# Two chained cross-attentions: transposes of x' in two parts, banks of the second and third picked keys exchanged, second queries copy before the normalisation of tiles 0 and 1

## What is computed

```python
# L0: 16 heads of 16 channels, 64 context rows; token t sees only the rows idx[t]-1, idx[t], idx[t]+1
q = split(rmsnorm(x, gamma_q) @ Wq.T); kn = rmsnorm(ctx, gamma_kv)
k = split(kn @ Wk.T); v = split(kn @ Wv.T)
w = where(|pos - idx| <= 1, relu(q k / sqrt(16))**2, 0)
x1 = x + (w / max(w.sum(), 1e-6) @ v) @ Wo.T
# L1: one head, softmax over 64 context rows, then residual and layer norm
q = gelu(x1' @ Wq + bq); k = gelu(ctx @ Wk + bk); v = gelu(ctx @ Wv + bv)
out = layernorm(softmax(q k) @ v @ Wf + bf + x1) * ln_gamma + ln_beta
```

## Time and profile before

| | |
|---|---|
| median of 3 runs | 343.87 us (343.45 to 344.19) |
| profiled execution | 343.76 us, of which 342.0 us is the span from first to last instruction |
| busy in the span | PE 324.4 (95%), DVE 287.9 (84%), ACT 250.8 (73%), POOL 231.9 (68%) |
| 60 to 302 us (steps 3 to 16) | PE 239.1 of 242.0 us busy, clock share 1.00 |

### The profile page before, as it was taken

One profiled execution on the slowest core, in us unless ns is written; L12 is line 12 of the kernel. 1 busy time (PEld: TensorE's weight loads), 2 busy tenths in 40 slices (PEclk: granted clock), 3 DMA queues, 4 the chain that ended last, 5 costly groups with the idle time before them and its releaser, 6 DMA issues.

```text
span 342.0 us, 5710 instructions
## 1 busy us (share of the span) xinstructions
PE 324.4 (95%) x1914; PEld 238.7 (70%) x1914; DVE 287.9 (84%) x456; ACT 250.8 (73%) x598; POOL 231.9 (68%) x233
## 2 busy tenths in 40 slices
PE   8999999999999999999999999999999999989980
PEld 3675678868686767776768687776768686857750
DVE  2789598888888888898988888898888888889766
ACT  4898524587878787969696969697887878785752
POOL 4416170246979696969788787878797969665414
PEclk9999999999999999999999999999999999999996
DMA  6987635934253433425261616162624242110103
GB/s 234 389 249 201 196 109 128 252 83 140 76 184 93 167 110 141 137 105 172 71 207 61 216 61 213 66 202 76 183 94 161 103 150 91 52 61 0 63 0 123
DMA packets 30268, 46.34 MB, mean 136 GB/s; under 512 B 2400, under 2 KB 16736, under 8 KB 30240
## 3 DMA queue, kind: packets, MB, share of 16 engines
q1 hardware_dynamic: 27264, 37.86, 36.0%
q0 software_dynamic: 2016, 7.34, 5.3%
q10 hardware_dynamic: 960, 0.79, 0.7%
HBM read 25.14 MB, written 8.39 MB: 98 GB/s over the span
## 4 chain that ended last, share of the span: by engine, by line
PE 76%; DVE 18%; issue 3%; ACT 2%; DVEq 0%
PE ps L532 12%; PE ps L533 12%; PE ps L534 12%; PE ps L583 7%; PE ps L577 6%; DVE qkp L1339 5%; PE ps L668 4%; PE ps L785 4%; PE ps L776 4%; PE ps L703 4%; PE ps L617 2%; PE ps L564 2%; DVE kv L1257 2%; PE ps L673 1%; PE ps L517 1%
## 5 line engine op out<-in xcount | busy, mean ns | idle before, releaser
L1293 DVE TENSOR_TENSOR qkp<-ps,bufs 128x1024 f32<-128x1024 f32 x48 | 56.0, 1219 | 9.3 <-ACT bufs L1035 8.0
L443 POOL TENSOR_TENSOR bufs<-bufs,lng_twice 128x1024 f32<-128x1024 f32 x14 | 33.7, 2408 | 27.2 <-ACT bufs L1074 25.1
L432 POOL TENSOR_TENSOR qkp<-qkp 128x1024 f32<-128x1024 f32 x15 | 35.9, 2396 | 21.6 <-DVE qkp L1304 21.6
L389 POOL TENSOR_TENSOR x_lo<-x_ring,x_hi 128x1024 fp32r<-128x1024 f32 x16 | 38.2, 2387 | 7.0 <-ACT x_hi L1031 7.0
L1112 ACT ACTIVATE xp_hi<-bufs 128x512 fp32r<-128x512 f32 x28 | 17.7, 634 | 31.9 <-DVE bufs L1381 31.9
L1304 DVE TENSOR_TENSOR qkp<-ps,wn 128x1024 f32<-128x1024 f32 x31 | 37.6, 1215 | 3.8 <-PE ps L583 3.7
L448 POOL TENSOR_TENSOR bufs<-bufs,lnb_row 128x1024 f32<-128x1024 f32 x14 | 33.5, 2395 | 0.1
L1035 ACT ACTIVATE bufs<-ps 128x512 f32<-128x512 f32 x32 | 19.2, 602 | 14.4 <-PE ps L534 14.4
L532 PE MATMUL ps<-x_hi,wh_q 128*128 128x512 f32 x64 | 26.7, 417 | 0.0
L1042 ACT ACTIVATE bufs<-bufs 128x256 f32<-128x256 f32 x64 | 25.7, 407 | 0.0
L1074 ACT ACTIVATE bufs<-ps,nbias,half_rstd 128x256 f32<-128x256 f32 x52 | 25.2, 566 | 0.3
(11 more groups left out here) (257 smaller groups left out, 920.2 us busy)
## 6 DMA issues: line engine op xcount, KB each, us to landing
x_ring<-xT SPq DMA_DIRECT2D x16, 512.0 KB, 3.4
bufs<-x SPq DMA_DIRECT2D x16, 512.0 KB, 5.0
out<-bufs POOLq DMA_DIRECT2D x14, 512.0 KB, 3.3
idx_ring<-idx SPq DMA_DIRECT2D x16, 256.0 KB, 4.1
wkv_lo<-kv SPq DMA_DIRECT2D x32, 126.0 KB
kvs<-kv SPq DMA_DIRECT2D x30, 126.0 KB
vfd<-bufs SPq DMA_DIRECT2D x8, 256.0 KB, 4.7
qkp<-ctxT SPq DMA_DIRECT2D x2, 512.0 KB, 6.7
```

The costliest lines, as they stand in the source:

```text
L389: G.tensor_tensor(x_lo[:, :, :], x_ring[:, e % RING, :, :], f32_view(x_hi[:, :, :]), ALU.subtract).then_inc(xl_ready, 2)
L432: G.tensor_tensor(att[:, 1, :, :], att[:, 0, :, :], att[:, 1, :, :], ALU.add).then_inc(pair_ready, 1)
L443: G.tensor_tensor(zo, zn, lng_twice[:, :].unsqueeze(1).broadcast_to([P, TT, D]), ALU.mult).then_inc(zg_ready, 1)
L1293: V.tensor_tensor(qk[:, s, :, :], ps[:, bank0:bank0 + 2, :], q0, ALU.mult).then_inc(qk_ready, 1)
```

## The change

Four edits, for the batches after the first:

- UP keys go to banks 0 and 1 and DOWN keys to 6 and 7. The waits follow the banks: UP keys wait for the weighting of the DOWN values (`att_ready`), DOWN keys for the normalisation (`zn_ready`).
- DVE's products read from the exchanged banks.
- The eight transposes of x' become two calls of `back`: tiles 0 and 1 (bank 6) ahead of the `scT` transposes, tiles 2 and 3 (bank 7) behind them. The first call now waits for the third key product (`3 * a + 3`) and no longer for the second.
- On ACT the copy of the second half of the first queries (`copy_q0(a, 1)`, L1035) stands ahead of the normalisation of tiles 0 and 1 and no longer behind it.

```diff
             def up_keys(a):
                 pe.wait_ge(kvs_in[a % 2], 64 * (a // 2 + 1))
-                picked_keys(a, UP, 6)
+                picked_keys(a, UP, 6 if a == 0 else 0)
...
+                def back(tiles):
+                    for j in tiles:
+                        for c in range(DC):
+                            mm(out_rows(j, c * P, P), xpT[:, c, j * P:(j + 1) * P], ident,
+                               is_transpose=True, start=(j % 2 == 0 and c == 0), stop=False, skip_group_check=True)
+
                 if b is not None:
                     queries1(0)
                 if a is not None:
-                    if n is not None:
-                        pe.wait_ge(zn_ready, 2 * n + 2)
-                    if f == 0:
-                        pe.wait_ge(k1_copied, 4)
+                    pe.wait_ge(att_ready, 3 * f + 2)
                     up_keys(a)
...
                 if a is not None:
-                    pe.wait_ge(att_ready, 3 * f + 2)
-                    picked_keys(a, DOWN, 0)
+                    if n is not None:
+                        pe.wait_ge(zn_ready, 2 * n + 2)
+                    if f == 0:
+                        pe.wait_ge(k1_copied, 4)
+                    picked_keys(a, DOWN, 6)
...
                     if a is not None:
-                        pe.wait_ge(qk_ready, 3 * a + 2)
+                        pe.wait_ge(qk_ready, 3 * a + 3)
                     else:
                         pe.wait_ge(zn_ready, 2 * n + 2)
-                    for j in range(TT):
-                        for c in range(DC):
-                            mm(out_rows(j, c * P, P), xpT[:, c, j * P:(j + 1) * P], ident,
-                               is_transpose=True, start=(j % 2 == 0 and c == 0), stop=False, skip_group_check=True)
+                    back((0, 1))
                     pe.wait_ge(scT_cp, b + 1)
                     for u in range(2):
                         i = nc.tensor.transpose(ps[:, 4, (2 + u) * P:(3 + u) * P], scT[:, u * P:(u + 1) * P], ident)
                     i.then_inc(sc_mm, 1)
+                    back((2, 3))
...
                 if n is not None:
                     normalise(range(2, TT))
-                if n is not None:
-                    normalise(range(0, 2))
                 if a is not None and f is not None:
...
                     copy_q0(a, 1)
+                if n is not None:
+                    normalise(range(0, 2))
...
                     multiply_keys(a, CENTRE, 2)
-                    multiply_keys(a, UP, 6)
-                    multiply_keys(a, DOWN, 0)
+                    multiply_keys(a, UP, 0)
+                    multiply_keys(a, DOWN, 6)
```

## The result

| | before | changed |
|---|---|---|
| median of 4 runs | 343.66 us (343.30 to 344.19) | 340.93 us (340.88 to 341.43) |
| ratio | | 0.9923 (95%: 0.9905 to 0.994) |
| profiled execution | 343.76 us, span 342.0 | 340.88 us, span 339.1 |

The median fell by 2.7 us where 2.4 were forecast. POOL's lines, L610 and L668 kept theirs.

What follows compares the result with a forecast made beforehand. PE was taken as the bound, losing 0.29 us a step at L668 to DVE's sum. 13 x 0.17 = 2.2 plus 0.15 in the tail make 2.4 us: 343.76 to 341.4 us, range 340.6 to 342.2 (chance 0.62).

Steps and rivals of the forecast that it cites:

- The wait at L668: PE loses 0.29 us a step waiting for DVE's sum; the split makes L668 0.17 us earlier a step.
- new stop: PE reaches the `scT` transposes before their copy is ready: 0.06 us wait plus 0.06 restart a step.
- The first rival: The gap at L668 is the cost of changing from 32 to 128 columns, not DVE's sum: 343.8 to 345.4 us.
- The third: Rival: the split is worth more because `scT` doesn't delay PE, 339.8 to 340.5 us; chance of more than forecast 0.05.
- The exchange and the copy at nothing: Bank exchange worth nothing by itself; ACT's earlier query copy gives back 0.10 us, swallowed in a 0.11 cover: value 0.
- POOL: POOL's sequence comes 0.26 us late each step but loses that again at L419 behind DVE's instruction: cost 0.
- signs of being wrong: Steps of 17.88 or more; L403 without idle time and L419 at 0.20; L1339 waiting for L432; L577's load waiting for L1304.
- The fourth rival: POOL becomes the bound if over about 0.5 us late at L419: 344.9 us; slower through POOL or PE's wait 0.09.
- The second rival: Late POOL L416 holds up DVE's L1384, delaying UP keys up to 0.1 us a step: 342.7 us, chance 0.05.
- The tail: After step 16 L802 stands in L668's place; ACT, idle 0.16 before rounding the transposed sums, gains that: 0.15 us.
- The cover of the copy's 0.49: POOL's sum L432, 0.49 us later, still ends 0.15 before L1339 wants it, with 0.14 more beyond that.

Runs made afterwards that it cites:

- kernel 5: The changed kernel with five of the eight x' transposes ahead of the `scT` transposes and three behind: 339.98 us, 0.9884 of the kernel before the change.
- kernel 1: The kernel before the change with the split of the transposes alone, banks, waits and ACT's order as they were: 340.69 us, ratio 0.9928.
- kernel 3: The changed kernel with ACT's copy of the queries again behind the normalisation of tiles 0 and 1: 340.97 us, 0.9938 of the kernel before the change.
- kernel 8: The changed kernel with two extra small POOL additions a step (0.31 us) ahead of L403: 342.07 us, 0.995 of the kernel before the change.
- kernel 9: The changed kernel with five extra small POOL additions a step (0.78 us) ahead of L403: 352.22 us, 1.0242 of the kernel before the change.
- kernel 7: The kernel before the change with the split and the copy ahead of the normalisation, but no exchange of banks: 346.56 us, ratio 1.0075.
- kernel 4: The changed kernel with POOL's one-time doubling of ln_gamma moved ahead of the first normalisation factors: 340.66 us, 0.9924 of the kernel before the change.
- kernel 2: The changed kernel with all eight x' transposes again ahead of the `scT` transposes: 343.46 us, 1.0011 of the kernel before the change.
- kernel 12: The changed kernel run once more, unaltered: 341.44 us, 0.9933 of the kernel before the change.

## Why the prediction was right, and where it was not

**The wait at L668.** Right in place and size. The distance from the first x' transpose to L668 fell by 2.96 - 2.78 = 0.18, where 0.17 was worked out. The `scT` pair's new stop was forecast at 0.06 + 0.06. Undisturbed, the pair would start 0.17 + 3 x 0.11 = 0.50 behind the first of the four transposes; it starts 193.05 - 192.50 = 0.55 behind, and the next transposes 0.28 behind it in place of 0.22: 0.05 + 0.06. That L668 could start at L610's modelled end, without its own price for the change of width, was taken from one row and holds (0.08 before the end). The first rival, in which the gap is the price of the width, is refuted, since the gap went from 0.22 to nothing at the same change of width. The third is refuted too: `scT` does delay PE, and kernel 5 shows what the split gives without that delay.

**The exchange and the copy at nothing.** Right in the steady steps. Kernels 1 and 3 reach 17.67 without the copy. DVE's gain ahead of the first product stops at the third, which waits 0.51 for the DOWN keys.

**POOL.** Right for the steady steps. L419 was forecast to start 0.26 behind DVE's instruction and to end 0.74 behind its start; it starts 0.25 and ends 0.74 behind. Of the signs of being wrong one was there by half (L403 has lost its idle time in the steady steps, but L419 is at 0.49 and not at 0.20) and one in a single step (L1343 waits for L432). The fourth rival, POOL as the bound, had its point of decision right in kind: kernel 8 stands about on it at 17.67, kernel 9 beyond. But its price was too low: when POOL passes the first half of DVE's pair it doesn't lose only the excess, it runs into the second half or puts L416 behind the first, and loses another 0.5. The second rival, L416 holding up DVE, didn't come about: in the step above L416 runs from 184.87 to 185.91, L1388 starts at 185.74, inside it, and its pair takes 1.48 as ever.

**The tail.** Forecast 0.15, measured 0.24. The other kernels with a split have 55.36 to 55.48, apart from kernels 7 and 9, which are slower there too, so some 0.2 to 0.3 are real. What is beyond the 0.15 I haven't traced.

**Terms that were missed.** Two, of opposite sign, and they cancel in the sum. That the sum came out as near as it did is luck to this extent, some 0.4 us either way.
First, the first normalising step was taken to be like the others. The cover of the copy's 0.49 was worked out in a steady step (0.15 before L1339, then 0.14), and the doubling L439, once 0.69 with its start, was not on the list. That step takes 18.17 where 17.71 had been counted: 0.46, and kernel 4 takes it away.
Second, each steady step is 17.67 and not 17.71, 11 x 0.04 = 0.4 us more gain. The difference doesn't lie where the change was costed: 0.18 of the 0.22 are between the x' transposes and L668, and the other 0.04 are between L668 and the next x' transposes, in matmuls whose order didn't change. Kernel 1 has it without the exchange or the copy, and kernel 2 without the split. Half of it, 0.02 in the mean, arises in the first matmuls L532 and L533 behind the UP keys. There the weight load waited 0.19 for the copy L1035, which the prediction put at nothing because loads run ahead. In the changed kernel and in kernel 2 this wait is gone. But kernel 1 still has it (2.4 us in 13 places) and has steps of 17.67 all the same, so it isn't shown to be the cause. What makes these distances shorter stays open.
With -0.43 at the start of the program, which is of the run and not of the change, the numbers close: 13 x 0.17 + 0.15 = 2.4 forecast; 2.45 measured behind the start, and 2.7 to 2.9 over all. The repeat on another chip, kernel 12, gave 343.52 - 341.44 = 2.1, so tenths of these differences of medians aren't to be read.

The Trainium skill (SBUF — State Buffer, "Who interferes with whom") says that a DVE instruction with two SBUF inputs and a POOL instruction which reads SBUF keep each other out until the one that began first has ended. Where DVE was first the rows agree that POOL is held up: 0.73 and 0.49 for 0.20 at L419, and 1.57 for 1.04 at L416 in kernel 9. They don't show it shut out until DVE has ended: L419 ends with DVE's instruction and not 0.20 behind it, and L416 loses 0.53 and not 0.72. Where POOL was first, L416 ahead of L1388, they don't, and the measurement decides: DVE wasn't held up.

## What to carry to other kernels

Where an engine that is the bound waits for a result, look at the chain that produces it: if the engine itself makes an early link of that chain and stands behind filler work, move just as much filler behind the link as lets its input be ready when the engine comes to it. Here the right cut was 5 and 3 of 8, worth 4.2 us, while 4 and 4 left a stop and 6 and 2 delayed the result again. A cover that is worked out in a steady step must be checked in the first and last ones, where work that is done once comes on top. And slack of an engine that comes from overlapping another's instruction has an edge: up to it lateness is free, behind it another instruction is met and, here, 0.5 us are lost at a stroke (kernel 8 in one step, kernel 9 in nearly all).

## What the runs showed of the hardware

- A small POOL addition (128x4) takes 0.20 us alone, and when it starts inside a DVE instruction with two SBUF inputs it ends with that instruction: 0.73, 0.49 and 0.30 us by how late it starts. POOL's power instruction L416 of the same size takes 1.04, and 1.57 when it starts 0.02 behind DVE; it is held up for 0.53 of the 0.72 that DVE's first half still runs. When it starts ahead of DVE, DVE isn't delayed.
- A stop of PE costs more than its length here: behind one the second matmul of 128 columns starts 0.17 and not 0.11 after the first, 0.06 us more. At the `scT` pair of the changed kernel the next transposes start 0.28 behind it (193.33 - 193.05); in kernel 5, which has no stop there, 0.22 (193.06 - 192.84).
- At the change from 64 to 128 columns the table of waits holds the same 5.4 us in 14 places for L749 as for L785, although the product asked for ended some 1.2 us ahead of L785 and ends 0.15 ahead of L749 (191.12 + 1.23 = 192.35, start 192.50). The table names DVE for it, but a release 1.1 us later leaves the wait as it was, so DVE isn't its cause.
